# Score chunks in halves of one bank each, and a third bank for VectorE's ring

## What is computed

```python
# h: normalised rows; 16 heads of 16 features
x = x + self_attention(h)        # softmax(q k^T / 4) v, then the output projection
x = x + cross_attention(h, ctx)  # the same against 120 rows of context
x = x + h @ w4bit + bias + h @ a @ b
x = x + sigmoid_attention(h)     # rotary q and k; sigmoid(q k^T / 4), divided by its sum, times v
x = x + one_head_cross_attention(h, ctx)
x = x + 0.5 * (h @ expert1 + h @ expert2)
```

## Time and profile before

| | |
|---|---|
| median of 3 runs | 1289.73 us (1287.9 to 1290.94) |
| the profiled execution | 1288.81 us, its span 1287.0 |
| TensorE matmuls busy | 1108.4 us, 86% |
| VectorE busy | 789.0 us, 61% |
| ScalarE busy | 637.0 us, 49% |
| GpSimd busy | 589.0 us, 46% |
| granted clock of TensorE, mean | 0.94 |

### The profile page before, as it was taken

How to read it: one execution, slowest core, us unless ns; L and a number is a source line. 1 busy time by engine, 2 the same in 40 slices (tenths; PEclk the granted TensorE clock), 3 DMA queues, 4 the chain that set the end, 5 groups by cost and what they waited for, 6 DMA issues and landing times. The chain is left out here.

```text
span 1287.0 us, 24305 instructions
## 1 busy us (share of the span) xinstructions
PE 1108.4 (86%) x8472; PEld 814.3 (63%) x8472; DVE 789.0 (61%) x1785; ACT 637.0 (49%) x1183; POOL 589.0 (46%) x854
## 2 busy tenths in 40 slices
PE   3426799999999998898888989999999997899975
PEld 2214567776776776666666657777777764677853
DVE  2605657676767645545556787878777752366761
ACT  1011456565656565545545345656666664454430
POOL 5063323333333344444445687777777711023343
PEclk8567799999999999989999999999999999899996
DMA  8044646464646334433434065756566760124455
GB/s 250 0 49 62 89 63 86 65 87 65 87 65 90 57 69 80 80 64 73 76 69 74 3 92 68 88 67 82 75 76 80 86 83 11 32 78 137 135 156 180
DMA packets 122502, 103.95 MB, mean 81 GB/s; under 512 B 26615, under 2 KB 122126, under 8 KB 122382
## 3 DMA queue, kind: packets, MB, share of 16 engines
q1 hardware_dynamic: 115502, 96.37, 45.6%
q10 hardware_dynamic: 6880, 6.03, 1.8%
HBM read 28.56 MB, written 4.19 MB: 25 GB/s over the span
## 5 line engine op out<-in xcount | busy, mean ns | idle before, releaser
L673 ACT ACTIVATE l_probs<-l_sT 128x1024 f32<-128x1024 f32 (+1 forms) x320 | 325.3, 1022 | 107.8 <-PE l_sT L910 55.9
L797 DVE TENSOR_REDUCE l_nmax<-l_ring 128x2 f32<-128x512 f32 (+1 forms) x384 | 253.4, 676 | 170.2 <-PE l_ring L941 168.5
L910 PE MATMUL l_sT<-qstack,kstack 99*128 99x256 bf16 (+2 forms) x1280 | 193.4, 274 | 4.6 <-ACT l_probs L673 4.5
L941 PE MATMUL l_ring<-kstack,qstack 96*128 96x256 bf16 (+1 forms) x1024 | 148.8, 251 | 40.5 <-DMA kstack<-l_kpart 19.5
L926 PE MATMUL l_o<-l_probs,v_heads 128*32 128x256 f32 (+1 forms) x2560 | 162.3, 386 | 1.1 <-ACT l_probs L673 0.9
L910 PEld LDWEIGHTS l_sT<-qstack,kstack 99*128 99x128 bf16 (+2 forms) x1280 | 126.7, 105 | 36.1 <-issue 8.0
L941 PEld LDWEIGHTS l_ring<-kstack,qstack 96*128 96x128 bf16 x1024 | 78.0, 99 | 96.4 <-issue 40.4
L991 PE MATMUL l_ring<-wT,l_zT 128*128 128x256 f32 x512 | 123.9, 385 | 0.6 <-DVE l_tokk L818 0.6
L926 PEld LDWEIGHTS l_o<-l_probs,v_heads 128*32 128x32 f32 (+1 forms) x2560 | 72.2, 110 | 64.3 <-issue 18.3
L1026 PE MATMUL l_ring<-wT,l_attnT 128*128 128x256 f32 x384 | 100.8, 392 | 11.5 <-DVE l_nmax L797 8.7
L973 PE MATMUL l_copy<-l_zT,wT 128*128 128x256 f32 x384 | 104.3, 403 | 1.8 <-ACT l_q L699 1.0
(11 more groups left out here) (196 smaller groups left out, 1956.1 us busy)
## 6 DMA issues: line engine op xcount, KB each, us to landing
qstack<-l_qpart SPq DMA_DIRECT2D x288, 128.0 KB, 4.2
kstack<-l_kpart SPq DMA_DIRECT2D x192, 128.0 KB, 5.7
t_experts<-in_experts SPq DMA_DIRECT2D x60, 256.0 KB, 3.0
kstack<-l_kpart SPq DMA_DIRECT2D x96, 60.0 KB, 3.4
x_res<-in_x ACTq DMA_DIRECT2D x4, 1024.0 KB, 11.2
out_y<-x_res SPq DMA_DIRECT2D x16, 256.0 KB, 3.7
l_cx<-in_ctx SPq DMA_DIRECT2D x16, 90.0 KB, 2.9
t_cx<-in_ctx SPq DMA_DIRECT2D x16, 90.0 KB, 3.0
```

Source lines behind the costliest of these rows:

```text
L673: act.activation(probs[g % 4][0:kp, :], sT[g % 2][0:kp, :], ACT.Sigmoid if sig(u) else ACT.Exp, scale=HD ** -0.5).then_inc(p_ok, 1)
L797: dve.tensor_reduce(nmax[u % 2][:, tt, h0:h0 + hb], bank("s", u, i)[:, 0:hb * sk].rearrange("p (h k) -> p h k", h=hb), AX_X, ALU.max, nega ...
L910: i = pe.matmul(sT[g % 2][0:kp, j * S:(j + 1) * S], kstack[u % SLOTS][0:rows_used, col * width(u) + kt * kp:col * width(u) + (kt + 1) * kp ...
L941: m = pe.matmul(out[:, j * sk:(j + 1) * sk], qstack[u % SLOTS][0:STACK, (h0 + j) * S + tt * P:(h0 + j) * S + (tt + 1) * P], kstack[u % SLO ...
```

## The change

The four banks of `sT` and two of `ring` become three of `sT` and three of `ring`. A chunk is filled as two halves of two matmuls, each half in one bank of 512 columns, and half n = 2g + (0 or 1) goes to bank n mod 3. ScalarE reads a chunk in two activations of 512 columns. Half n waits for the exponential of half n - 3; before, chunk g waited for chunk g - 2. Ring job n waits for job n - 3 instead of n - 2. In all three tables pv2 and pv3 (of the unit before) move ahead of sT1, and the s that stood between them moves in front of or behind them. The number of matmuls, of DMAs and of all other jobs is as before; TensorE raises `sT_ps` twice a chunk, and ScalarE `p_ok`.

```diff
@@ ORDERS @@
     "self": """
-        np sT0 s qa s qb p0q dq0 s sT1 s pv2 e0 pv3 o1 e1 s
+        np sT0 s qa s qb p0q dq0 s pv2 pv3 sT1 s e0 o1 e1 s
         ka s kb p0k dk0 oT1 sT2 s e2 p1q dq1 p2q dq2 sT3 e3 nT p1k dk1 s p2k dk2 va rows vb s
         pv0 pv1 o0 s aT s sT4 e4 s z cl s sT5 e5 oT0 xb s
         sT6 e6 pa st fac cx pb s sT7 e7 s""",
     "cross": """
-        np sT0 qa qb p0q dq0 sT1 s pv2 e0 pv3 o1 e1 s
+        np sT0 qa qb p0q dq0 pv2 pv3 s sT1 e0 o1 e1 s
...
     "sigmoid": """
-        sT0 qa qb rope_q sT1 p0q dq0 pv2 e0 pv3 o1 e1 ka kb rope_k
+        sT0 qa qb rope_q p0q dq0 pv2 pv3 sT1 e0 o1 e1 ka kb rope_k
         sT2 p1q dq1 p0k dk0 fr oT1 e2 sT3 va vb rows p1k dk1 p2q dq2 e3
         pv0 pv1 o0 aT p2k dk2 sT4 fxb st fz e4 sT5 pa z pb e5 xb
         sT6 fst fac ffac qT e6 fa fb sT7 oT0 kT e7""",
@@ banks @@
-        sT = [ctx.enter_context(nc.psum_tensor(f"l_sT{i}", [P, 4 * S], F32)) for i in range(2)]
-        ring_bank = [ctx.enter_context(nc.psum_tensor(f"l_ring{i}", [P, 512], F32)) for i in range(2)]
+        sT = [ctx.enter_context(nc.psum_tensor(f"l_sT{i}", [P, 2 * S], F32)) for i in range(3)]
+        ring_bank = [ctx.enter_context(nc.psum_tensor(f"l_ring{i}", [P, 512], F32)) for i in range(3)]
@@ ScalarE, exponentials @@
-                act.wait_ge(sT_ps, g + 1)
...
-                act.activation(probs[g % 4][0:kp, :], sT[g % 2][0:kp, :], ACT.Sigmoid if sig(u) else ACT.Exp,
-                               scale=HD ** -0.5).then_inc(p_ok, 1)
+                for half in range(2):
+                    n = 2 * g + half
+                    act.wait_ge(sT_ps, n + 1)
+                    act.activation(probs[g % 4][0:kp, half * 2 * S:(half + 1) * 2 * S], sT[n % 3][0:kp, :],
+                                   ACT.Sigmoid if sig(u) else ACT.Exp, scale=HD ** -0.5).then_inc(p_ok, 1)
@@ TensorE, ring_slot and scores @@
-                if n >= 2:
-                    pe.wait_ge(ring_empty, n - 1)
-                return ring_bank[n % 2]
+                if n >= 3:
+                    pe.wait_ge(ring_empty, n - 2)
+                return ring_bank[n % 3]
...
-                if g >= 2:
-                    pe.wait_ge(p_ok, g - 1)
...
+                for half in range(2):
+                    n = 2 * g + half
+                    if n >= 3:
+                        pe.wait_ge(p_ok, n - 2)
+                    for j in range(2):
+                        h = 4 * group + 2 * half + j
...
+                    i.then_inc(sT_ps, 1)
```

More of the change, by code:

```diff
@@ L548, in stack_rows @@
                 if w + str(part) in ("q0", "k0") and u >= SLOTS:
-                    sp.wait_ge(sT_ps, last_chunk(u - SLOTS) + 1)
+                    sp.wait_ge(sT_ps, 2 * last_chunk(u - SLOTS) + 2)
                 ready = second_ok[w] if part == 1 else (first_ok if part == 0 else third_ok)[w][sig(u)]
@@ L766, in bank @@
             def bank(job, u, i=0):
-                return ring_bank[ring[job, u, i] % 2]
+                return ring_bank[ring[job, u, i] % 3]
             def filled(job, u, i=0):
@@ L903, in scores @@
                         pe.wait_ge(n_dma, 16 * (u + 1))
-                if g >= 2:
-                    pe.wait_ge(p_ok, g - 1)
                 group, kt = c * 4 // chunks_of(u), c % (chunks_of(u) // 4)
-                for j in range(4):
-                    h = 4 * group + j
-                    col = h % HH * KT + h // HH
-                    i = pe.matmul(sT[g % 2][0:kp, j * S:(j + 1) * S],
-                                  kstack[u % SLOTS][0:rows_used, col * width(u) + kt * kp:col * width(u) + (kt + 1) * kp],
-                                  qstack[u % SLOTS][0:rows_used, col * S:(col + 1) * S], start=True, stop=True)
-                i.then_inc(sT_ps, 1)
+                for half in range(2):
[4 more added lines that the diff above has]
+                        h = 4 * group + 2 * half + j
+                        col = h % HH * KT + h // HH
+                        i = pe.matmul(sT[n % 3][0:kp, j * S:(j + 1) * S],
+                                      kstack[u % SLOTS][0:rows_used, col * width(u) + kt * kp:col * width(u) + (kt + 1) * kp],
+                                      qstack[u % SLOTS][0:rows_used, col * S:(col + 1) * S], start=True, stop=True)
+                    i.then_inc(sT_ps, 1)
             def times_values(u, group):
@@ L923, in times_values @@
                     g = chunk["sT", u, group * per + kt]
-                    pe.wait_ge(p_ok, g + 1)
+                    pe.wait_ge(p_ok, 2 * g + 2)
                     for j in range(4):
@@ L985, in project_tokens @@
                     return
-                out = ring_bank[ring[job, u, 0] % 2]
+                out = ring_bank[ring[job, u, 0] % 3]
                 kq = SC if from_context else P
@@ L1023, in project_out @@
                     ring_slot("pb", u)
-                out = ring_bank[ring["pb", u, 0] % 2]
+                out = ring_bank[ring["pb", u, 0] % 3]
                 for k in range(KT):
@@ L1034, in linear @@
                     ring_slot("fb", b)
-                out = ring_bank[ring["fb", b, 0] % 2]
+                out = ring_bank[ring["fb", b, 0] % 3]
                 for k in range(KT):
```

## The result

| | before | after |
|---|---|---|
| median of 8 runs each | 1287.53 us (1284.07 to 1290.94) | 1295.88 us (1292.81 to 1297.84) |
| ratio, 95% interval | | 1.0059 (1.0041 to 1.0078) |
| the profiled execution, its span | 1288.81, 1287.0 | 1295.91, 1294.1 |

The change costs 8.35 us. The forecast was 1298, 8.3 above the median that it started from. Over the whole span it looks like little, but it is a gain and a loss in different stages. I read both traces by periods (from one aT to the next: L1017 before, L1021 after) and added them up by kind. Each row is one profiled execution: a steady cross or sigmoid period repeats to 0.02 us from one kernel to another, while the self periods and the two ends do not.

A forecast was written before the change was run, and what follows sets the result against it. TensorE, 88 to 97% busy with an in-order queue, was taken to bound the kernel. 34.6 + 1.7 - 20 - 7.5 - 0 gave 8.8 us more: 1297.6 profiled, 1298 as median, range 1286 to 1311.

The forecast's parts named there:

- The halves, sigmoid: Sigmoid order: second halves wait for exponentials queued behind ScalarE's copies; 34.6 us lost, bounds 25 and 40.
- ScalarE's load: All chunks: two half exponentials replace each whole one; ScalarE's busy time grows by 53 us, beside TensorE's work.
- The cross periods: Ten cross periods without linear stage: third ring bank removes TensorE's waits for VectorE, 2.0 each; 20 us gained.
- With the linear layer: Six cross periods with the linear stage: 1.25 gained each, as fb then waits for pb's residual; 7.5 us gained.
- Self: Self periods: loop of kstack copies and kb absorbs the ring's gain; 0, bounds 0.5 gained in each of 14, 0.3 lost.
- what is won is lost: Self periods: time won ahead of the next unit's first s is lost waiting there for kstack copies; net 0.
- pv2 and pv3 ahead of sT1: Orders of all three kinds: the move adds no wait, since both pv jobs need no ring bank; zero.
- The sum: Whole kernel: 34.6 + 1.7 - 20 - 7.5 - 0 makes 8.8 us more.
- Ring gain wins: Rival: self periods gain 0.5 each, mixed cross periods 2.0; 1287, or 1277 with exposed halves at low bound; chance 0.15.
- The cross periods don't shrink: Rival: kstack copies or GpSimd's chain hold cross periods at 17 us, half the gain goes; 1312; chance 0.12.
- They cancel: Rival: sigmoid waits come out near the low bound; 1290 to 1292; chance 0.13.
- The increments cost: Rival: TensorE's 320 more semaphore increments cost 0.02 or 0.03 each where exposed; 1306; chance 0.03.

The follow-up runs named there:

- e1: Changed kernel with ScalarE's exponentials of the sigmoid order moved ahead of the copies in front of them; 1264.37 us, ratio to before 0.9795.
- e2: Changed kernel with only the exponential behind kT's copy in the sigmoid order moved ahead of that copy; 1279.40 us, ratio 0.9909.
- e3: Changed kernel with only the exponential behind fz's copy in the sigmoid order moved ahead of that copy; 1283.55 us, ratio 0.9945.
- e5: Kernel before with chunks in halves, four in flight in its four sT banks, two ring banks and its old orders; 1285.41 us, ratio 0.9979.
- e7: Kernel before with the last three of six kstack copies in self units from the fifth on cut to one partition of 16; 1283.25 us, ratio 0.9962.
- e4: Changed kernel, VectorE's ring back at two banks; 1328.65 us, ratio 1.0291. In "e4's first half" it is instead ScalarE's exponential job for sT4.
- e8: Changed kernel with the last three of six kstack copies in self units from the fifth on cut to one partition of 16; 1287.72 us, ratio 0.9992.
- e9: e1 with ka and kb (and p0k, dk0) moved ahead of two row maxima in the self order; 1256.99 us, ratio 0.9758.
- e6: Kernel before, whole chunks and two ring banks, with only the changed orders (pv2 and pv3 ahead of sT1); 1283.96 us, ratio 0.9957.
- e0: Not a run: ScalarE's exponential job for chunk sT0, which needs the probs buffer that pv2 uses; it has no measured kernel time.
- e10: e9 with ka and kb one row maximum earlier still in the self order; 1260.81 us, ratio 0.9783.

## Why the prediction held, term by term

- **The halves, sigmoid: 34.6 forecast, 35.7 measured.** The places cost what was worked out. From start to start in the trace of after: 1.12 behind kT, 1.12 behind fz, 0.25 behind z, 0.69 for sT5 directly behind sT4, 1.12 for qT directly before sT7. e1 took back 32.9 us of the periods, where the four kinds of place that it touches make 14.6 + 11.2 + 3.0 + 3.4 = 32.2; e2 and e3 took back single ones. The arithmetic rested on the 594 ns copy as the stand-in for a half; the halves took 604 as a mean. By the Trainium skill ("ScalarE: Activation LUTs", section "What ACT_TABLE_LOAD costs") a half would take 613, an estimate from its 186 ns and 0.833 ns a column; the 604 lie between that and the copy's 594. One sign was misread: I had said that these waits show as 0.85 us idle, three times a period. They show as 0.96, twice. Idle time counts from the modelled end, 0.27 after a start, but the next matmul would have started 0.11 after it, so 0.16 of a delay is hidden and not 0.27, and the 0.25 behind z leaves 0.09, which the list does not show. Of e2's 16.3 us, 14.6 was the forecast; the rest is in one of the last periods, which fell by 2.7 (22.25 to 19.51) instead of 1.1.
- **ScalarE's load: mis-sized, without effect.** I had 53 us more; it is 20.6 for the exponentials (345.9 against the 325.3 of the earlier trace rows) and 15.3 in all (652.3 against 637.0). Two halves in a row overlap: 1.08 for a pair at 900.55, while two of 0.604 would be 1.21. I had said that overlaps were not taken off, but not that they take off more than half.
- **The cross periods: 20 forecast, 22.2 measured, apart from the clock.** A period went from 17.01 to 14.83, 2.2 for the 2.0 I kept. I had added up idle times here, and start times in the self periods. By starts, in one period of before and one of after, pa comes 0.80 sooner behind the job in front of it, oT0 0.89, the s behind nT 0.40 and the values 0.16, together 2.25; sT1's second half takes the foreseen 0.1 back. The table says 25.4, but 3.2 of that belong to before: two of its cross periods took 18.46 and 18.76 at a granted clock of 0.91, so in part at the lower level of 1.2 GHz, behind three periods of the same work at the upper one; e5 and e7, with the same waits and no such stretch, have 170.5. The row of that stretch in before (columns as in the earlier trace rows):

```profile
540.30:577.52 37.22, 33.31 (x258) 24.07 (x257) 17.85 (x42) 17.91 (x34) 15.51 (x28) 0.91 0.36 70
```

- **With the linear layer: 7.5 forecast, 7.5 measured** (125.4 to 118.0, rounded), and e4 has them back at 125.3. The sum is hit, not each period: the six gain 2.0, 1.2, 1.4, 0.7, 0.6 and 1.7 for the 1.25 that I kept. The wait that I named as taking over is there: from 640 to 790 fb (L1041) waits four times for the residual, 3.0 us in all.
- **Self: 0 forecast, 2.5 gained.** The loop of copies and kb is real: e7 and e8 shortened the copies and e9 the other side, and all three paid about what was foreseen (4.1 for 5, 7.4 for 8, 5.6 for 5.5). The step that failed is "what is won is lost": a wait that varies from 0.02 to 1.06 us absorbs a shift only in the units where it is long. With 0.46 to hide and a mean wait of 0.36, some of it gets through: 0.19 a period. The 2.5 itself is uncertain by about 1 us: the thirteen periods take 276.0 to 277.3 in before, e5 and e6, and 274.8 to 275.6 in after, e1, e2 and e3. The last two periods in that order lost 1.3 instead of 1.7.
- **pv2 and pv3 ahead of sT1: zero forecast.** In the kernel before it is a gain of 3 us, in three of the last four periods (e6). I looked there only for waits that the halves add, and took the earlier trace rows, a unit in which ScalarE idles 1.79 us for pv2, for the duration of e0 alone. How much of it survives in the changed kernel, where the halves need the order, was not tried apart.
- **The sum.** The terms as measured give 35.7 + 1.3 - 22.2 - 7.5 - 2.5 = 4.8 us more, for 8.8 forecast, and the medians 8.35 (interval 5.3 to 10.0). Between the profiles lie 3.4 us more ahead of the first aT and 2.0 at the end, against the 3.2 of clock. The ends have no changed instruction in them but the first ramp of the layers stage; they vary between 176.7 and 182.2, and 202.7 and 207.2, over these kernels. Whether the changed kernels are later there by a part of it or by chance stays open. That the medians differ by almost what was forecast is therefore luck in part: the mechanism and the two large terms are shown, but the sum of the terms misses the forecast by 4 us. What makes up for it was in no term: 2.2 in the profiles (5.4 at the ends less the 3.2 of clock), and 1.3 between the profiled executions and the medians.

**The rivals.** *Ring gain wins* needed 9 us more gain than I kept; it came to 2.5 in the self periods and 2.2 in the cross periods. With the copies shortened in both kernels the change gains 5.8 us in the self periods (e7 and e8, 273.2 to 267.4): the rival's 0.5 a period is nearly there, behind the copies. *The cross periods don't shrink*: nothing took over, TensorE is 99% busy there. *They cancel*: the waits weren't near the low bound. *The increments cost*: e5 rules them out for this kernel. The Trainium skill ("TensorE: Matmul & The Clock Gate", section "The cost: per-tile semaphore tail") charges some 26 ns for each increment in a pack of tiles. By that figure 320 of them would be 8 us, and the eight of a sigmoid period 0.2, both estimates. Here, with one increment behind two matmuls in a row instead of four, e5 shows no such charge: its steady periods are as long as before within 0.01.

## What to carry to other kernels

Splitting a buffer so that more pieces are in flight makes each piece wait for a nearer one. Ask of each place which instruction must now have run that hadn't before, and what stands ahead of it in its engine's queue: here a copy of 0.6 us ahead of an exponential, at three places of a period, cost most of 36 us, and moving the exponential past it turned a change that lost 0.6% into one that gains 2%. A wait that varies from unit to unit is a cushion only where it is long; to see what a gain in front of it is worth, shorten what it waits for, as e7 and e8 did, and the gain shows in full (0.46 a period for 0.19). And when a job must be moved to avoid a deadlock, price its new place for every engine that waits for it, not only for the one that it might hold up.

## What the runs showed of the hardware that I had not expected

- Two ScalarE instructions of 512 columns in a row out of PSUM take 1.08 us, not twice 0.604: in the 349 such pairs of after the second starts 0.48 after the first (median), 0.11 before it ends. Against one of 1024 columns at 1.022, the split costs ScalarE 0.06 a chunk. The Trainium skill ("ScalarE: Activation LUTs", section "What ACT_TABLE_LOAD costs") gives 93 ns for the overlap of back-to-back activations; the trace shows some 20 ns more, and the measurement decides.
- From the end of a half to the start of the matmul that waited for it: e4's first half starts at 900.55 and lasts about 0.60, the matmul starts at 901.20, so 0.05 us. In all 43 such waits of over 0.3 us in after it is 0.053 to 0.056.
- 320 more semaphore increments on TensorE, and as many waits, cost nothing visible: 17.01 or 17.02 us for a cross period of 17.01, 20.84 for a sigmoid period of 20.84 (e5).
- A ring bank's way through VectorE is 1.26 us for a reduction of 0.68: first matmul at 275.75, reading from 276.17, next matmul into the bank at 277.01 (e10). Three banks filled in 0.66 don't cover it.
